# Wide attentions with row maxima in quarters and logits ten heads behind the scores, bulk stores issued by ScalarE, and norm scales spread by transposes

## The reference, cut to what matters

```python
q = (x @ Wq.T + bq).reshape(b, -1, 16, 8)
k = (ctx @ Wk.T + bk).reshape(b, -1, 16, 8)
v = (ctx @ Wv.T + bv).reshape(b, -1, 16, 8)
scores = jnp.einsum('blhd,bLhd->bhlL', q, k) / jnp.sqrt(8)
scores = jnp.where(mask, scores, -jnp.inf)   # in layer 0's only
out = jnp.einsum('bhlL,bLhd->blhd', softmax(scores), v).reshape(b, -1, 128)
out = out @ Wo.T + bo
```

## Time and profile before

| | us |
|---|---|
| median of 3 runs | 1614.13 (1611.19 to 1616.87) |
| profiled execution | 1604.65, span 1602.9 |
| masked wide attention, first score to last sum | about 198 to 424 |
| unmasked wide attention | about 952 to 1153 |
| TensorE clock granted, mean | 0.953 |

### The profile page before, as it was taken

How to read it: one execution, slowest core, us unless ns; L and a number is a source line. 1 busy time by engine, 2 the same in 40 slices (tenths; PEclk the granted TensorE clock), 3 DMA queues, 4 the chain that set the end, 5 groups by cost and what they waited for, 6 DMA issues and landing times. The chain is left out here.

```text
span 1602.9 us, 30499 instructions
## 1 busy us (share of the span) xinstructions
PE 1422.3 (89%) x10976; PEld 711.8 (44%) x11002; DVE 991.9 (62%) x1940; ACT 804.8 (50%) x1498; POOL 456.0 (28%) x656
## 2 busy tenths in 40 slices
PE   7988999999999999778987898889978788978887
PEld 5766634444364444346643452222335333523344
DVE  5776598887262221465557679999285666456646
ACT  4554537667533333214440045777754466446637
POOL 7122300000004565320136330000021456235621
PEclk9999999999999999889997899999986999999988
DMA  2000552111300000001000074321100531143100
GB/s 103 2 0 0 158 175 86 46 48 27 121 0 1 0 0 1 0 7 46 12 7 1 0 206 142 88 58 45 34 1 9 178 99 43 60 156 97 46 1 27
DMA packets 82394, 85.46 MB, mean 53 GB/s; under 512 B 7244, under 2 KB 67916, under 8 KB 81772
## 3 DMA queue, kind: packets, MB, share of 16 engines
q1 hardware_dynamic: 82296, 84.18, 17.1%
HBM read 51.06 MB, written 32.51 MB: 52 GB/s over the span
## 5 line engine op out<-in xcount | busy, mean ns | idle before, releaser
L1337 ACT ACTIVATE arena<-ps 128x1024 f32<-128x1024 f32 x256 | 262.1, 1024 | 109.3 <-PE ps L1244 108.7
L1229 PE MATMUL ps<-k_stack,q_stack 49*128 49x512 bf16 x512 | 190.5, 382 | 14.8 <-DVE small L1360 12.5
L1244 PE MATMUL ps<-q_stack,k_stack 51*128 51x256 bf16 x1024 | 189.4, 272 | 0.6 <-ACT arena L1337 0.4
L1357 DVE CUSTOM_DVE_ANT_0 small<-ps,mask_b 128x512 bf16<-128x512 f32 x256 | 168.0, 689 | 29.7 <-PE ps L1229 28.2
L1360 DVE TENSOR_REDUCE small<-ps 128x1 f32<-128x512 f32 x256 | 161.9, 684 | 16.0 <-PE ps L1229 14.9
L1546 DVE TENSOR_REDUCE small<-ps 128x6 f32<-128x768 f32 x128 | 122.6, 958 | 75.9 <-PE ps L1426 73.4
L1256 PE MATMUL ps<-arena,v_pad 128*32 128x256 f32 x2048 | 162.3, 391 | 1.1 <-ACT arena L1337 1.1
L1523 ACT ACTIVATE arena<-ps 128x384 f32<-128x384 f32 x256 | 118.0, 488 | 77.5 <-PE ps L1448 76.7
L1134 POOL TENSOR_SCALAR_AFFINE_SELECT arena<-arena 128x256 f32<-128x256 f32 x256 | 101.8, 406 | 85.9 <-ACT arena L1523 85.5
L2678 POOL TENSOR_TENSOR arena<-arena 128x512 f32<-128x512 f32 x64 | 79.7, 1266 | 92.5 <-ACT arena L2573 92.5
L2604 DVE TENSOR_TENSOR arena<-ps,arena 128x512 f32<-128x512 f32 x64 | 44.2, 691 | 99.7 <-PE ps L2521 98.8
(11 more groups left out here) (357 smaller groups left out, 2936.3 us busy)
## 6 DMA issues: line engine op xcount, KB each, us to landing
q_stack<-q_scratch SPq DMA_DIRECT2D x128, 96.0 KB
k_stack<-k_scratch SPq DMA_DIRECT2D x64, 192.0 KB
k_scratch<-arena SPq DMA_DIRECT2D x8, 768.0 KB, 3.9
k_stack<-k_scratch SPq DMA_DIRECT2D x64, 96.0 KB
q_scratch<-arena SPq DMA_DIRECT2D x4, 1152.0 KB, 7.1
arena<-in_ctxT SPq DMA_DIRECT2D x8, 512.0 KB, 6.4
k_scratch<-arena SPq DMA_DIRECT2D x8, 512.0 KB, 4.7
k_scratch<-arena SPq DMA_DIRECT2D x16, 256.0 KB, 4.2
```

The costliest lines, as they stand in the source:

```text
L1229: pe.matmul(ps[:, t, :], c.q_stack[par][64 * e:64 * e + ROW_MAX, pr, t * P:(t + 1) * P], c.k_stack[par][64 * e:64 * e + ROW_MAX, pr, :], s ...
L1244: mm = pe.matmul(ps[:, bank, (ch % 2) * S:(ch % 2 + 1) * S], c.k_stack[prv][64 * e:64 * e + ROWS, pr, ch * P:(ch + 1) * P], c.q_stack[prv] ...
L1337: act.activation(buf.probs[i % 8], ps[:, bank:bank + 2, :].rearrange("p a n -> p (a n)"), ACT.Exp, scale=scale).then_inc(g["probs"].sem, 1)
L1357: dve.tensor_tensor_reduce(buf.junk[t], ps[:, t, :], c.mask_b[:, M_X + t * SC:M_X + (t + 1) * SC], 1.0, FLOOR, op0=ALU.add, op1=ALU.max, a ...
```

## The change

- `norm_spread` uses `pe.transpose` of the broadcast column with the identity instead of an f32 product with it.
- Wide attentions handle maxima by quarters of 4 heads: four negations, splits, turns, copies and placements per batch. `max_rows` has four places, and the turned rows lie in the upper half of bank 6 or 7.
- Logits of head `j` run in slot `j + 10`, so heads 0 to 5 of a batch share a step with its own scores, and heads 6 to 15 follow in the next step's first ten slots. Sums run 5 slots behind the logits, as before. Quarter q is turned in slot 6, 10, 14 and (next step) 2, and is wanted four slots later.
- ScalarE waits for the parts and issues the q stores and the first bulk k store. SyncE has a new order of loads, stores and placements.
- ScalarE's copies of sums stand at the end of slots 3, 7, 11 and 15.

```diff
-    c.max_rows = sb("max_rows", [16, 2 * S], BF16)
+    c.max_rows = sb("max_rows", [16, 4 * S], BF16)
...
-        mm = c_matmul(pe, out[:, j * P:(j + 1) * P], rstd[:, j:j + 1].to_broadcast([P, P]), c.ident[:, :])
+        mm = pe.transpose(out[:, j * P:(j + 1) * P], rstd[:, j:j + 1].to_broadcast([P, P]), c.ident[:, :])
...
+AV_BEHIND = 5
+BEHIND = 10
+TURN = 6
...
+def wide_transfers(c, buf, sp, made):
+    g = c.sig
+    def load(b, hf):
+        if b > 1:
+            sp.wait_ge(g["logits"].sem, g["logits"].at((b - 2) * H + H // 2 * (hf + 1)))
+            sp.wait_ge(g["stored_q"].sem, g["stored_q"].at(STORES))
+            sp.wait_ge(g[f"stored_k{b // 2}"].sem, g[f"stored_k{b // 2}"].at(STORES))
+        load_stacks(c, sp, b % 2, hf, b * S, b * SC, SC)
+    def place(s, q):
+        sp.wait_ge(g["turned_out"].sem, g["turned_out"].at(s * GROUPS + q + 1))
+        for e in range(2):
+            sp.dma_start(c.q_stack[s % 2][64 * e + ROW_MAX:64 * e + ROWS, 2 * q:2 * q + 2, :],
+                         buf.maxrow[q][4 * e:4 * e + 4, :]).then_inc(g[f"max_placed{q}"].sem, 16)
+    for hf in range(2):
+        load(1, hf)
+    for s in range(B + 1):
+        if s:
+            place(s - 1, 3)
+            if s + 1 < 4:
+                store_parts(c, sp, "k", SC, s + 1, s + 2, g[f"stored_k{s + 1}"].sem)
+            if s + 1 < B:
+                load(s + 1, 0)
+        if s < B:
+            place(s, 0)
+            place(s, 1)
+            if 0 < s and s + 1 < B:
+                load(s + 1, 1)
+            place(s, 2)
...
+def wide_turn(c, buf, pe, q, s, par, first, kept):
+    g = c.sig
+    if kept is not None:
+        out = g[f"summed_out{q % 2}"]
+        pe.wait_ge(out.sem, out.at(kept))
+    pe.wait_ge(g["negmax"].sem, g["negmax"].at(s * GROUPS + q + 1))
+    if not (first and q < 2):
+        pe.wait_ge(g["turned_out"].sem, g["turned_out"].at(s * GROUPS + q - 1))
+    for t in range(2):
+        mm = pe.transpose(wide_turned(c, q)[:, t * P:(t + 1) * P],
+                          buf.parts[par][:, q, t, :, :, :].rearrange("p e a r -> p (e a r)"), c.ident_b[:, :])
+    mm.then_inc(g["turned"].sem, 1)
...
     (TensorE's step)
             for i in range(H):
+                j = (i - BEHIND) % H
+                own = i >= BEHIND
+                b, prv, here = (s, par, front) if own else (s - 1, 1 - par, back)
+                start = first and not (own and par)
+                if here and j % 4 == 0:
+                    placed = g[f"max_placed{j // 4}"]
+                    pe.wait_ge(placed.sem, placed.at((b + 1) * 32))
-                if back and i == 3:
-                    turn_max(c, buf, pe, 1, b, prv, first, b * 2 if before else None)
-                if front and i == 11:
-                    turn_max(c, buf, pe, 0, s, par, first and par == 0, b * 2 + 1 if back else None)
+                if back and i == TURN - 4:
+                    wide_turn(c, buf, pe, 3, s - 1, 1 - par, False, (s - 1) * 2 if before else None)
+                if front and i in (TURN, TURN + 4, TURN + 8):
+                    q = (i - TURN) // 4
+                    wide_turn(c, buf, pe, q, s, par, first and par == 0, (s - 1) * 2 + 1 + q // 2 if back else None)
...
     (a sum group's first piece)
-                sum_waits(c, pe, grp, b, first, front)
+                if grp < 2 or front:
+                    pe.wait_ge(g["turned_out"].sem, g["turned_out"].at(b * GROUPS + grp + 3))
...
     def scalar(act):
         act.activation(c.small[:, 648:649], c.consts[:, C_EPS:C_EPS + 1], ACT.Exp)
+        act.wait_ge(g["parts"].sem, g["parts"].at(made.parts))
+        store_parts(c, act, "q", SC, 1, B // 2, g["stored_q"].sem)
+        store_parts(c, act, "k", SC, 1, 2, g["stored_k1"].sem)
...
     (VectorE)
-                if n % H == H - 1:
+                if n % 8 == 7:
                     dve.wait_ge(g["maxed"].sem, g["maxed"].at(s * NSCORE + n + 1))
-                    dve.tensor_scalar(buf.nm[par][:, hf, :, :, :], buf.mx[par][:, hf, :, :, :], FLOOR, -1.0, ALU.max, ALU.mult)\
+                    dve.tensor_scalar(buf.nm[par][:, q, :, :, :], buf.mx[par][:, q, :, :, :], FLOOR, -1.0, ALU.max, ALU.mult)\
```

More of the change, by code:

```diff
@@ L1028, in __init__ @@
         self.ones = sm[:, 640:640 + HALF]
+        if wide:
+            self.maxrow = [c.max_rows[:, i * S:i * S + S] for i in range(GROUPS)]
+            self.mx, self.nm = ([fold(sm[:, at + 32 * i:at + 32 * i + 32], (GROUPS, 2, 2, 2)) for i in range(2)] for at in (0, 160))
+            self.parts = [fold(sm[:, 288 + 32 * i:320 + 32 * i].bitcast(BF16), (GROUPS, 2, 2, 2, 2)) for i in range(2)]
 def attend_steps(nc, engine, body, unrolled=False):
@@ L1200, in sum_waits @@
         pe.wait_ge(g["turned_out"].sem, g["turned_out"].at(b * 2 + 2 + grp // 2))
+AV_BEHIND = 5
[29 more added lines that the diff above has]
+            place(s, 2)
+    for q in range(GROUPS):
+        sp.wait_ge(g[f"max_placed{q}"].sem, g[f"max_placed{q}"].at(32 * B))
@@ new lines, in wide_pool, with step @@
+def wide_pool(c, buf, pool, nch, made):
+    g = c.sig
+    pool.memset(buf.ones, 1.0).then_inc(g["cleared"].sem, 1)
+    pool.wait_ge(g["cleared"].sem, g["cleared"].at(1))
+    pool.wait_ge(g["v_kept"].sem, g["v_kept"].at(made.values))
+    def step(it, par, front, back, before):
+        s = it * 2 + par
+        if back:
+            wide_split(c, buf, pool, s - 1, 3, 1 - par)
+        if front:
+            if before:
+                pool.wait_ge(g["summed"].sem, g["summed"].at((s - 1) * GROUPS))
+            pool.tensor_copy(c.v_pad[par][:, 0:nch, :, 0:DH],
+                             buf.vt[:, bass.ds(s * (SC // P), nch), :].rearrange("p c (h d) -> p c h d", h=H))\
+                .then_inc(g["v_padded"].sem, 1)
+            for q in range(3):
+                wide_split(c, buf, pool, s, q, par)
+    attend_steps(c.nc, ENG.Pool, step)
@@ L1203, in attend_wide, with wide_keep_max @@
+def wide_keep_max(c, buf, act, s, q, first):
+    g = c.sig
+    placed = g[f"max_placed{q}"]
+    act.wait_ge(g["turned"].sem, g["turned"].at(s * GROUPS + q + 1))
+    if not first:
+        act.wait_ge(placed.sem, placed.at(s * 32))
+    act.activation(buf.maxrow[q][0:8, :], wide_turned(c, q), ACT.Identity).then_inc(g["turned_out"].sem, 1)
 def attend_wide(c, masked, made):
@@ L1285, in step @@
                     score_unit(i, 0, s, par, first)
-                if back:
-                    mm = logit_half(i, 1, prv)
+                if here:
+                    mm = logit_half(j, 1, prv)
                     if masked:
                         mm.then_inc(g["half_masked"].sem, 1)
[L1290 to L1297, removed]
+                n = (i - BEHIND - AV_BEHIND) % H
+                if i >= BEHIND + AV_BEHIND:
+                    if front:
+                        sum_piece(n // 4, n % 4, s, par, first and par == 0, True)
+                elif back:
+                    sum_piece(n // 4, n % 4, s - 1, 1 - par, first, front)
+                if here and masked:
+                    pe.wait_ge(g["half_masked"].sem, g["half_masked"].at((b * H + j) * 2 + 2))
                     logit_mask(i, 1, e, False)
@@ L1301, in step @@
                     score_unit(i, 1, s, par, first)
-                if back:
-                    logit_half(i, 0, prv).then_inc(g["logits"].sem, 1)
-            if not front:
-                for n in range(H - LATE, H):
-                    sum_piece(n // 4, n % 4, b, prv, False)
+                if here:
+                    logit_half(j, 0, prv).then_inc(g["logits"].sem, 1)
         pe.wait_ge(g["v_kept"].sem, g["v_kept"].at(made.values))
```

90 lines of the change are left out of this document (52 added, 38 removed).

## The result

The changed kernel took 1600.41 us (median of 20 runs, 1584.64 to 1612.86), the kernel before 1612.94 us on the same chips (20 runs). The ratio is 0.993, 95% interval 0.9907 to 0.9953: 11 us less, 8 to 15. It leaves out five slow executions of the changed kernel (1609.06 us and more); with them the ratio of the means is 0.994, 9 us less. The prediction was 1601 us, 13.5 us less than the kernel before. Its profiled execution took 1598.23 us.

The account below looks back on a forecast made before the run. TensorE, busy 1422.3 of 1602.9 us, was taken as the bound, with VectorE setting the pace where only scores run. Norms -14.6 and attentions +1.1 gave -13.5 us: from 1614.13 to 1600.6, say 1601 us, range 1588 to 1617.

Parts of the forecast that it names:

- Part 4, norms: Norm spreads by transposes instead of products: 0.43 us saved a spread, -14.6 us in all, bounds -10.3 and -20.6.
- The pitch: In norm spreads, time from one TensorE record to the next: 0.112 us for products, 0.117 us for transposes.
- 34 exposed spreads: In the norms, 34 of 48 spreads were counted as shortening the path, bounds 24 and 48.
- the second rival: The clock falls in seven norms without filler or projections between variance and spread: 21 us, 1622 us; chance 0.16.
- Part 1, slots: Wide attentions, logits ten heads behind instead of sixteen: -7.2 us masked, -7.1 us unmasked.
- Part 2, turns: Wide attentions by quarters: more turns cost +6.7 us masked, +3.0 us unmasked; more negations +3.2 us unmasked.
- VectorE's chain still feels the transposes: Unmasked attention: a turn was taken to cost 0.3 us, between 0.22 and 0.42.
- the added negation: Unmasked attention: sixteen more negations on VectorE at 0.2 us each, +3.2 us, or 0 if they fall in gaps.
- Part 3, transfers: Waits for placements in the wide attentions: 1.5 us for both first placements, +1 us later, +2.5 us together, bounds 0 and +9.
- the first rival: Late placements: the small transfer doesn't pass the bulk stores, +9 instead of +2.5 us, 1609 us; chance 0.14.
- The attentions' sum: Slots, turns, negations and transfers of both wide attentions: -0.5 - 0.9 + 2.5 = +1.1 us, bounds about -13 and +11.
- the third rival: Attentions gain what slots promise: turns at 0.22 us, negations free, -13 us at most, half likelier, 1594 us; chance 0.14.

Follow-up runs that it names:

- e1: The kernel before with only the norm spreads made of transposes, attentions as before: 1601.88 us, ratio 0.9943 to before.
- e2: The changed kernel with norm spreads by f32 products again, so only the attentions and their transfers are changed: 1610.39 us, ratio 0.9995 to before.
- e11: The changed kernel with three fillers, not two, in slots with scores alone, six ahead of the slot 10 wait, and a later k store: 1596.65 us, ratio 0.9891.
- e12: The kernel e11 with norm spreads by f32 products, as in the kernel before: 1603.97 us, ratio 0.9942 to before.
- e4: The changed kernel with an appended stage of TensorE work only: fillers, then stretches of products, transposes, variances or two in turn; its total time means nothing.
- e7: The changed kernel with four transposes instead of two in each turn of the wide attentions: 1598.17 us, ratio 0.9927 to before.
- e6: The changed kernel with the bulk stores issued by SyncE again, ahead of its first placement: 1608.37 us, ratio 0.9979 to before.
- e8: The changed kernel with three fillers instead of two ahead of each head with scores alone: 1601.75 us, ratio 0.9934 to before.
- e9: The changed kernel with the first step's k store issued after ScalarE's first copy of maxima: 1602.09 us, ratio 0.994 to before.

## Why the prediction was right, and where it was not

That the time was met to 1 us is luck in part. The change was forecast as -13.5 and measured as -11 us, and the kernel before came out 1.2 us under the 1614.13 that the forecast started from. Behind the sum stand two terms that erred in opposite directions and a clock that took something back from both.

**Part 4, norms: -14.6 forecast, about -9 measured** (e1 -9; after against e2 -10; e11 against e12 -8). The pitch and the 34 exposed spreads were right at full clock. If one takes each norm's shortest time in the traces with transposes (nine of twelve at 1.00), the sum is about 163 us, 15 less than before's 178.6, and the shortest of the three traces with products (before, e2, e12) sum to 178.3. The step that failed is that the clock stays: the second rival was true in part. In three of the twelve norms (at 709, 781 and 1217 us after) it falls in all nine traces with transposes throughout and no filler; in others only in some. At its lowest clock a norm is up to 3.5 us longer than in the trace where it is shortest, and the norms' sum is 165.7 to 174.1 us instead of 163. Part of this is not the change's: e2, with products, fell to 0.72, 0.74 and 0.78 in three norms, and its norms sum to 189.2 us. e4 shows the mechanism apart from waits. The rival named seven norms without projections; one of the three that always fall, at 1217 us, has projections. Its size, 21 us, was too large: the sum lies 3 to 11 us above 163, and a norm with a fall can still be shorter than with products (10.9 us at 0.84 against 11.9 at 1.00, the one at 781 us).

**Part 1, slots:** not measured by themselves; they stand in the attentions' sum. The masked attention, which kept its clock after, agrees with it: -7.2 for slots, +3.3 for turns and +1.2 of waiting are -2.7 us, and its part went from 249.3 to 246.6 us.

**Part 2, turns.** Masked 0.31 us against 0.42: 31 x 0.31 - 15 x 0.42 = +3.3 us instead of +6.7. Unmasked a steady quarter is 5.53 us instead of 5.8, over 20 of them 5.4 us less than forecast. Those of the second step take 5.70 to 5.71 us even at full clock, and two later ones 6.12 and 6.46 (e11). The failed step is the 0.3 us of "VectorE's chain still feels the transposes" or the 0.2 us of the added negation: the two together measure 0.21, and VectorE's waits for scores shrank from 10.3 to 2.8 us in 110. e7 speaks for the first. The wait on ScalarE's copy at a turn, 5.3 us in 14 times before, is gone, as forecast. Waits of TensorE in the unmasked attention before:

```profile
PE ps L1157 <- ACT arena L1316: 5.3, 14, 0.4
```

By e7 an added pair of transposes costs 0.11 us masked and 0.06 unmasked. The rest of a turn's price is then wait; that other work fills in around the transposes is argued and not shown.

**Part 3, transfers:** the waits were 3.2 us against 2.5, and the first rival is refuted by the changed kernel: the placement was there at 211.7 us, while the DMA engines moved 409 GB/s at 210 to 212 us and were done only at 214, and e6 shows its price, had it been true. What was missing is what follows the wait: about 1 us of idle TensorE in a stretch with little work was followed by up to 17 us at 1.2 GHz. That costs the masked attention about 4 us: from the norm ahead of it to the norm behind, 246.4 to 247.5 us in the traces without a fall, 248.7 to 253.6 with one, 249.3 before. For the unmasked one it is less clear: 219.3 to 220.0 without one in the first step, 219.5 to 226.6 with one, 224.8 before.

**The attentions' sum:** +1.1 forecast. At full clock they are 2 and 5 us shorter, by the traces, and 9 us (5 to 14) by e12's ratio; with the fall the changed kernel keeps about 1 to 2 of that. So the third rival (attentions some 6 us better than forecast) was right for the unmasked half, and the fall hid it.

**The range** held: 1600 lies near its middle. The chance of "faster" was added up wrongly: 0.56 + 0.14, half of 0.14 and a fifth of 0.16 are 0.80 and not 0.76.

By the fourfold factor for FP32 of the Trainium skill ("TensorE: Matmul & The Clock Gate", section Terms) the norm at 436 us would save an estimated 4 x (0.90 - 0.22) = 2.7 us. It gave 1.9; the measured factor of about two stands.

Open: why two first steps fell before slot 10; why the norm at 1217 us isn't held by filler; and some 2 us by which the unmasked attention is less short than its quarters say.

## What to carry to other kernels

Where a change lets TensorE wait just once in a stretch that is thin already, price also the stretch behind it at half the clock, and put filler ahead of the wait, no longer than the wait, so that it delays nothing. Making TensorE's work shorter can cost clock: where the neighbours are products of one column, the shorter operation may take away what held it. Here a small transfer passed bulk stores on another queue, at twice its quiet time; put behind them on their queue it took 9.1 us.

## What was not expected of the hardware

- One-column f32 products, TensorE busy throughout, dropped the granted clock from 1.00 to 0.50; f32 transposes alone held 1.00 over 15 us (e4).
- A wait of TensorE at slot 10, 0.8 to 1.3 us long (2.9 and 5.4 in e6), was followed by 3 to 17 us at 0.50 in 14 of 16 cases (not in the masked attentions of the changed kernel and e8, with waits of 1.2 and 0.9 us). With bf16 filler up to the wait the clock held there all six times.
- Issuing six bulk DMAs held ScalarE's queue for 1.87 and 4.96 us, three each, back to back; issued 6 us behind the first three, the last three held it for 1.56 us (e9, masked). A placement of a few rows took 5.5 us beside them instead of 2.5.
